# The attention residual of a two-layer kernel: added by TensorE in the projection's bank and written back by ScalarE

## The reference

```python
x = x + cluster_attention(_ln_c(x))     # _L0_conv_ref: f, v, 2x2 fold, 4 centres per fold, sigmoid
                                        # similarity, argmax mask, aggregate, 1x1 projection
t = _to_tokens(x)
t = t + ffn(_ln_t(t))                   # 96 -> 384 -> 96; operands rounded to 8-bit floats, sums to float16
x = _from_tokens(t, x)
```

## Time and profile before

| | |
|---|---|
| median of 3 runs | 3662.53 us (3660.05 to 3663.72) |
| the profiled execution's own time | 3659.49 us |
| its span, first to last instruction | 3657.6 us |
| first phase | up to about 1960 us of the span |
| TensorE clock granted, mean | 0.946 of 2.4 GHz |

### The profile page before, as it was taken

How to read it: one execution, slowest core, us unless ns; L and a number is a source line. 1 busy time by engine, 2 the same in 40 slices (tenths; PEclk the granted TensorE clock), 3 DMA queues, 4 the chain that set the end, 5 groups by cost and what they waited for, 6 DMA issues and landing times. The chain is left out here.

```text
span 3657.6 us, 68122 instructions
## 1 busy us (share of the span) xinstructions
PE 3017.4 (82%) x21990; PEld 1910.0 (52%) x21990; DVE 3218.4 (88%) x8131; ACT 2781.3 (76%) x6274; POOL 1728.9 (47%) x2404
## 2 busy tenths in 40 slices
PE   6787888878787878887876799997888888888887
PEld 5565665656565656565654344443444444444444
DVE  4888889898989898989886699999899999999998
ACT  2577777777777877777778455554799999999998
POOL 3777777777787877787864000000222222222221
PEclk9999999899999999999987899999999999999999
DMA  3233323232323232323212888897676667666762
GB/s 68 53 89 74 91 71 88 71 88 70 88 71 88 71 88 71 88 71 88 71 56 69 212 238 234 236 280 212 172 199 188 181 185 200 184 184 193 199 177 83
DMA packets 696178, 478.92 MB, mean 131 GB/s; under 512 B 407217, under 2 KB 674422, under 8 KB 683830
## 3 DMA queue, kind: packets, MB, share of 16 engines
q1 hardware_dynamic: 695830, 474.58, 49.2%
HBM read 272.09 MB, written 201.92 MB: 130 GB/s over the span
## 5 line engine op out<-in xcount | busy, mean ns | idle before, releaser
L1891 POOL TENSOR_SCALAR C_var<-C_st 128x16 f32<-128x16 f32 x64 | 13.5, 211 | 1338.6 <-DVE C_st L178 1338.6
L1464 DVE SCALAR_TENSOR_TENSOR B_y<-B_mid,B_coefs,B_y 128x512 f32<-128x512 f32 x768 | 509.0, 750 | 3.2 <-ACT B_y L1429 3.2
L1395 PE MATMUL B_ps_row<-B_z,B_band 128*128 128x512 f32 x1152 | 499.1, 596 | 15.1 <-DMA B_band<-edge_scratch 15.1
L378 DVE TENSOR_SCALAR A_hq<-A_h,A_b 128x512 f16<-128x512 f16 x768 | 319.4, 456 | 176.5 <-ACT A_h L370 169.6
L370 ACT ACTIVATE A_h<-A_hid 128x512 f16<-128x512 f32 x768 | 428.3, 594 | 59.5 <-PE A_hid L357 57.1
L178 DVE BATCH_NORM_STATS2 A_st<-A_xT 128x6 f32<-128x192 f32 x1536 | 443.6, 349 | 29.3 <-ACT A_xT L861 16.0
L370 ACT ACTIVATE C_h<-C_hid 128x512 f16<-128x512 f32 x768 | 425.0, 589 | 22.9 <-PE C_hid L357 22.5
L1504 ACT ACTIVATE C_q<-C_xT,C_shift,C_rstd 128x96 fp8e5<-128x96 f32 x1024 | 392.6, 457 | 43.3 <-POOL C_shift L1898 43.2
L894 ACT ACTIVATE A_xc<-A_xT,A_shift,A_rstd 128x96 f32<-128x96 f32 x1024 | 379.3, 456 | 4.2 <-POOL A_shift L1207 4.0
L167 POOL TENSOR_TENSOR A_rstd<-A_var,A_expo 128x16 f32<-128x16 f32 x128 | 376.5, 2941 | 10.7
L1395 PEld LDWEIGHTS B_ps_row<-B_z,B_band 128*128 128x128 f32 x1152 | 218.8, 190 | 294.2 <-issue 287.8
(11 more groups left out here) (167 smaller groups left out, 7248.7 us busy)
## 6 DMA issues: line engine op xcount, KB each, us to landing
A_xq<-in_x SPq DMA_DIRECT2D x32, 1536.0 KB, 8.9
x_scratch<-A_xT SPq DMA_DIRECT2D x64, 768.0 KB, 3.2
x_scratch<-A_x3h SPq DMA_DIRECT2D x64, 768.0 KB, 5.4
B_z<-x_scratch SPq DMA_DIRECT2D x96, 512.0 KB
y_scratch<-B_y SPq DMA_DIRECT2D x96, 512.0 KB, 3.6
C_x3q<-x_scratch SPq DMA_DIRECT2D x32, 1536.0 KB, 9.1
C_xT<-x_scratch SPq DMA_DIRECT2D x64, 768.0 KB, 16.6
C_y3q<-y_scratch SPq DMA_DIRECT2D x31, 1536.0 KB, 15.6
```

Source lines behind the costliest of these rows:

```text
L378: r = dve.tensor_scalar(self.hq[:, b, s], self.h16[:, b, s], self.w["b1"][:, j:j + 1], 0.0, ALU.add, ALU.max)
L1395: m = pe.matmul(bank(c, h), band[c.buf(NB)][:, d, :], z[c.buf(NB)][:, half(h), d:d + W], start=(d == 0), stop=(d == 2))
L1464: dve.scalar_tensor_tensor(y, mid[c.buf(2)][:, half(h), t:t + W], coefs[:, c.n, 3 + t:4 + t], y, ALU.mult, ALU.add).then_inc(ev["sums"], 1)
```

## The change

PE adds the residual itself: a second matmul, with the identity as its stationary and xT as its moving operand, accumulates onto the projection in the bank. ACT copies the bank over xT; its place is behind norm3 and ahead of fwd in the same slot. DVE's `x1` is gone. DVE's statistics of these chunks are done one slot later (`OUT_AT.get(s - 1)`: slots 4 to 7). On POOL pool_norm(q1, 1) now stands ahead of ln2(q1, 1).

```diff
                 bank_free(front, i, "out", k)
-                pe.matmul(front.bank("out", k)[:, 0:CW], simT[q.buf(2)][:, k, :], pabd[:],
-                          start=True, stop=True).then_inc(ev["out_full"], 1)
+                bank = front.bank("out", k)[:, 0:CW]
+                pe.matmul(bank, simT[q.buf(2)][:, k, :], pabd[:], start=True, stop=False)
+                pe.matmul(bank, ident, xT[q.buf(NB)][:, k * CW:(k + 1) * CW], start=False, stop=True).then_inc(ev["out_full"], 1)
...
+            def x1(q, k):
+
+                act.wait_ge(ev["out_full"], ev.at("out_full", q, k))
+                act.activation(xT[q.buf(NB)][:, k * CW:(k + 1) * CW], front.bank("out", k)[:, 0:CW],
+                               ACT.Copy).then_inc(ev["x1"], 1)
+
...
+                    for k in OUT_AT.get(s, ()):
+                        if q1.real:
+                            x1(q1, k)
                     for k in FWD_AT.get(s, ()):
...
-            def x1(q, k):
-
-                dve.wait_ge(ev["out_full"], ev.at("out_full", q, k))
-                v = xT[q.buf(NB)][:, k * CW:(k + 1) * CW]
-                dve.tensor_tensor(v, front.bank("out", k)[:, 0:CW], v, ALU.add).then_inc(ev["x1"], 1)
...
-                    for k in OUT_AT.get(s, ()):
-                        if q1.real:
-                            x1(q1, k)
                     for k in FWD_AT.get(s, ()):
                         if q4.real:
                             bn(q4, k, "xT", "bn1", st1)
-                    for k in OUT_AT.get(s, ()):
+                    for k in OUT_AT.get(s - 1, ()):
                         if q1.real:
                             bn(q1, k, "x1", "bn2", ff.st)
...
                 if q1.real:
+                    ff.pool_norm(pool, q1, 1)
                     ln2(q1, 1)
-                    ff.pool_norm(pool, q1, 1)
```

## The result

The changed kernel takes 3794.38 us (median of 4 runs, 3793.21 to 3795.28), the kernel before 3661.29 us in the same comparison. The ratio is 1.0363, 95% interval 1.0345 to 1.0380: slower by 133 us.

What follows compares the result with a forecast made beforehand. The step was taken as bound by leg A (DVE) plus leg B (POOL). A: -5.2 + 5.3 + 0.4, B: +3.5, together +4.0 us x 30 = +120, giving 3782 us; 8 in 10 for 3670 to 3835.

Steps and rivals of the forecast that it cites:

- The two legs: First-phase step of 60.0 us: leg A on DVE, first cosine to similarity(1), 31.9 us; leg B on POOL, to next cosine, 28.0.
- Leg A, -5.2 us of work: DVE, cosine to similarity(1): four x1 pairs gone, -4.1 us; bn2 of chunks 6 and 7 moved past its end, -1.1.
- Leg A, +5.3 us of waits: DVE, slots 3 to 6: its saved time turns into waits for ACT and PE, +5.3 us a step.
- Leg A, collision +0.4 us: Slot 6: later pool_norm(q1, 0) on POOL runs into DVE's similarity(1), costing 0.8 us at most; half taken, 0.4.
- The slot walk: Slots 3 to 6: half-clock PE in slot 3 delays `out` and ACT; DVE waits, ending at 832.3 us for 832.2.
- Leg B, +1.6 us for the wait: POOL after similarity(1): ln2 waits for slot 7's bn2 of chunk 7, ready at 6.0 us; ln1 starts at 9.2.
- Leg B, collision to +3.5 us: Slot 7: pool_norm beside DVE's hidden(7) and y(6) delays bn2 to 7.9 us, ln1 to 11.1; +3.5 us in all.
- Sum: Whole step: -5.2 + 5.3 + 0.4 on DVE's leg, +3.5 on POOL's; +4.0 us, x 30 = +120 us; chance 0.45.
- R1: Rival, faster: lead hides PE and ACT; DVE's leg loses 5.2 us, POOL's gains 3.5; -51 us, 3611; chance 0.14.
- R2: Rival, half the loss: no collision or a partial lead; +0.6 to +2.5 us a step, 3680 to 3737; chance 0.23.
- R4: Rival, no change: DVE's saving happens to equal POOL's loss, within 7 us in all; chance 0.06.
- R3: Rival, the clock: PE at half clock in slot 6 every step, costing 1.7 us more; 3833; chance 0.12.

## Why the prediction was right

3782 was forecast, 3794 measured. By its steps:

- **The two legs.** Held. Leg B moved 4.6 us with POOL's wait, leg A 0.1 us, and the time followed.
- **Leg A, -5.2 us of work.** Right in kind, too large by 0.5: x1 and the statistics are gone from the leg, but their records overlap the next operation's by 0.1 us each time, and over 25 steps of the kernel before they took 3.7 + 1.0 = 4.7 us of DVE's time.
- **Leg A, +5.3 us of waits.** The waits for ACT grew by 4.0 - 0.3 = 3.7 us.
- **Leg A, collision +0.4 us.** L1051, the similarity's two-input operation that the prediction described (1.25 us for 0.43 at 813.70), costs 0.6 us as a mean, between the 0.4 taken and the 0.8 "in full". DVE's busy time fell by 3.6 us and not by 4.7, so 1.1 us came on top in all. Besides L1051, 0.3 us is the third L378 of slot 3, beside pool_norm(i, 3), which the prediction left as before. The rest is small stretches and waits below 0.15 us.
- **Leg A in all.** Forecast +0.5, measured +0.1. That it came so close is luck: the work was 0.5 us too large, the waits 1.6 us too large and what came on top 0.7 us too small, and these nearly cancel.
- **The slot walk.** Its places were right: DVE waits for ACT's hidden pieces in slots 4 and 6 and for fwd. Its cause in slot 3 was only partly right, since a higher clock gave back 0.5 us of 3.0 in the kernel with the residual alone.
- **Leg B, +1.6 us for the wait.** Shown by the old order put back: the statistics are there 6.0 us after the similarity.
- **Leg B, collision to +3.5 us.** The term that was mis-sized: +4.6. L382 doubled (0.5 us), so the statistics came at 8.2 and not 7.9; the power behind them took 3.2 us for 2.9, so ln1 started at 11.8 for 11.1; and from ln1 to the inverse norms POOL took 20.9 us for 20.4.
- **Sum.** Forecast 4.0 us a step over 30 steps, measured 4.6 over 29. The 12 us between forecast and measurement flatter the sum a little, since leg A was 0.4 us too long in it and leg B 1.1 us too short.
- **R1** fell with leg A. Its idea had something in it: for slots 5 and 6 alone the lead does hide PE and ACT, and that kernel gains 1.8%.
- **R2** and **R4** fell with the time.
- **R3** didn't come. It expected slot 6 at half clock in every step; there `out` ran at half clock (0.64 us per instruction) in 10 of 25 steps before, and in none of 25 after (0.32). The granted clock of the first phase is 0.93, and 0.92 to 0.93 before.

## What to carry to other kernels

Cut a periodic schedule into the legs between releases and price a change by leg. A statistic put a slot later looks free on its own engine, but the power behind it on another engine was on the path, and the wait cost more than the work that was moved. When an engine gets faster, ask not only what it waits for next but what it now runs beside: here a DVE that came earlier moved under POOL's norm. Look at that too before you read a delay: the powers that were to move POOL's norm held DVE themselves. And move work by the slot: the two pairs in the slots where PE and ACT had idled gave 1.8%, the other two lost 0.6%.

## What the runs showed of the hardware

A DVE operation that starts within 0.2 us of POOL's norm can be held until POOL's four instructions are over: L249 3.52 us for 0.35, L378 3.18 for 0.35. L1041, 1.99 for 0.43, began as the second of the four was ending and was held to the end of the others. More often an operation takes two to three times its length (0.98, 1.07); what decides between the two isn't shown. POOL's power of 96x4 values stretched DVE too (L378 1.04 for 0.35 at 580.57, 0.11 us after the power had begun), while L249 took its usual 0.35 at 833.88 beside the power of 128x16. Statistics are not stretched (8 in 2.22 us beside pool_norm at 811.13), and neither is x1 with its PSUM operand (1.01 at 826.59). The Trainium skill (GPSIMD Engine Reference, Key points) names the contention, for two SBUF inputs or a 2-port mode. Beside POOL's norm these runs agree for the operations with two SBUF inputs (L249, L253, L1041) and for the two kinds that were left alone. L378 and L382 read one tensor and are hit too; in which mode they run no trace here shows. The runs show besides that one operation can be held for 3 us.

More work on PE in slots 5 and 6 raised its granted clock from 0.92 to 1.00 in the first phase; the same work in slots 3 and 4 left it at 0.93 to 0.95. With late statistics and no work added to PE it fell to 0.88.
